# A two-layer attention block and feed-forward: new orders for the first and last periods, feed-forward weights loaded elsewhere in the period, output weight rows in 12 transfers

## The reference

```
h1 = layernorm(x);  x = attention(h1, h1)      @ o1 + o1_b + x     # "own" attention, keys 100
h2 = layernorm(x);  x = attention(h2, context) @ o2 + o2_b + x     # "cross" attention, keys 361
h3 = layernorm(x);  a, g = split(h3 @ ff_w1 + ff_b1)               # 320 -> 2 x 1280
out = (a * gelu(g)) @ ff_w2 + ff_b2 + x                            # 1280 -> 320
```

## Time and profile before

| | |
|---|---|
| median of 3 runs | 1327.53 us (1322.02 to 1328.48) |
| the profiled execution, its own time | 1335.46 us |
| its span, first to last instruction | 1333.7 us |
| TensorE busy (matmul) | 1248.4 us, 94% of the span |
| VectorE, ScalarE, GpSimd busy | 62%, 50%, 45% |
| mean granted TensorE clock | 0.971 |
| stages (from the trace) | first stage to 150.1, lead-in to 199.0, 29 periods to 891, run-out to 973.4, feed-forward to 1333.7 us |

### The profile page before, as it was taken

The page is one execution under the profiler, slowest core; times in us unless marked ns, Lnnn a source line. Parts: engine busy times, 40 slices in busy tenths (PEclk is TensorE's granted clock), DMA queues, the critical chain, the costliest instruction groups (busy, mean ns, idle before and its releaser), DMA issues. The chain is left out here.

```text
span 1333.7 us, 34303 instructions
## 1 busy us (share of the span) xinstructions
PE 1248.4 (94%) x12788; PEld 1168.4 (88%) x12788; DVE 826.6 (62%) x1606; ACT 672.8 (50%) x1622; POOL 602.7 (45%) x792
## 2 busy tenths in 40 slices
PE   6999679999999999999999999998689999999999
PEld 4899578899988898888889999987589999999999
DVE  5645458888787787777787888875445333242521
ACT  5655236666665666656666666664343232313131
POOL 5521225555555554544655555541366342333331
PEclk9999789999999999999999999998689999999999
DMA  4576644545545555445454554533011101010000
GB/s 125 192 250 231 184 144 124 157 135 149 162 129 161 162 150 181 145 140 179 135 155 142 146 164 128 171 100 87 13 55 41 45 1 50 0 49 0 25 1 25
DMA packets 105865, 154.49 MB, mean 116 GB/s; under 512 B 21500, under 2 KB 87284, under 8 KB 105716
## 3 DMA queue, kind: packets, MB, share of 16 engines
q1 hardware_dynamic: 105716, 152.49, 37.4%
HBM read 62.98 MB, written 28.93 MB: 69 GB/s over the span
## 5 line engine op out<-in xcount | busy, mean ns | idle before, releaser
L1419 ACT ACTIVATE probs<-expin 120x400 f32<-120x400 f32 (+2 forms) x635 | 297.4, 506 | 133.1 <-PE expin L812 130.2
L1096 DVE TENSOR_REDUCE neg_max<-score 100x2 f32<-100x722 f32 x320 | 287.7, 899 | 105.9 <-PE score L786 104.7
L812 PE MATMUL expin<-qs,ks 128*120 128x200 f32 (+2 forms) x1270 | 201.4, 273 | 1.2 <-ACT probs L1419 0.9
L786 PE MATMUL score<-ks,qs 128*100 128x362 f32 x640 | 170.3, 348 | 29.4 <-DMA qs<-q_parts 13.8
L812 PEld LDWEIGHTS expin<-qs,ks 128*120 128x120 f32 (+2 forms) x1270 | 180.4, 183 | 11.3 <-ACT probs L1419 7.8
L2654 DVE SCALAR_TENSOR_TENSOR hidden<-ps_a,b_cols,gelu 128x320 f32<-128x320 f32 x100 | 55.0, 550 | 174.2 <-PE ps_a L2578 174.1
L1610 POOL MEMSET qs<- 128x2400 f32 (+1 forms) x58 | 112.6, 1942 | 94.9 <-PE expin L812 94.9
L2816 POOL TENSOR_TENSOR hid_lo<-hidden,hid_hi 128x320 fp32r<-128x320 f32 x100 | 88.2, 882 | 121.8 <-ACT hid_hi L2724 121.6
L190 POOL TENSOR_TENSOR scaled_heads<-turned_heads,rden 128x320 f32<-128x320 f32 x63 | 48.0, 762 | 190.2 <-DVE rden L195 190.2
L786 PEld LDWEIGHTS score<-ks,qs 128*100 128x100 f32 x640 | 87.4, 168 | 50.0 <-issue 40.2
L2736 ACT ACTIVATE gelu<-ps_g,b_cols 128x320 f32<-128x320 f32 x100 | 52.8, 528 | 137.6 <-PE ps_g L2578 137.6
(11 more groups left out here) (222 smaller groups left out, 2971.0 us busy)
## 6 DMA issues: line engine op xcount, KB each, us to landing
ks<-kc_parts SPq DMA_DIRECT2D x96, 362.0 KB, 3.7
qk_dram<-qk_parts SPq DMA_DIRECT2D x32, 500.0 KB, 5.3
qs<-q_parts SPq DMA_DIRECT2D x192, 75.0 KB
ks<-qk_dram SPq DMA_DIRECT2D x96, 125.0 KB
ctx_raw<-in_ctxT SPq DMA_DIRECT2D x64, 180.5 KB
ks<-kc_parts SPq DMA_DIRECT2D x96, 90.5 KB, 2.7
qs<-qk_dram SPq DMA_DIRECT2D x64, 125.0 KB
v_dram<-v_rows SPq DMA_DIRECT2D x32, 132.8 KB
```

The costliest lines, as they stand in the source:

```text
L786: mm = pe.matmul(score[0:N, a, 0:JP], qs[2][u][:, a, q_slot(c), :], ks[2][u][:, k_slot(c), :], start=True, stop=True)
L812: mm = pe.matmul(dst, ks[a][u][:, k_slot(c) if a == 2 else c, j0:j0 + n], qs[a][u][:, :, q_slot(c) if a == 2 else c, :], start=True, stop= ...
L1096: ins = nc.vector.tensor_reduce(dst, src, AX_X, ALU.max, negate=True)
L1419: nc.scalar.activation(probs[e % NPT][0:n, :], expin[e % 2][0:n, 0:HG * N], ACT.Exp, scale=SCALE)\
```

## The change

Nothing that is computed changes. Four things are done:

1. `rows_of_heads`: the rows of o1 and o2 go to the same places in 12 transfers of 32 partitions (40 KB), not 24 of 16 (20 KB).
2. `lead_in` has another order on all five engines, and `FILL_WORK` with it.
3. `load_w1` is issued inside the period, behind `place_max(2, x)`, not at its end. The rest of the period is as before.
4. `run_out` has another order on all five engines, and `DRAIN_WORK` with it.

```diff
 def rows_of_heads(w):
     pieces = []
-    for k, f0, step in ((0, 0, 4 * DH), (2, P, 4 * DH), (1, 2 * P, 0)):
-        for i in range(HG):
-            for half in range(2):
-                f = f0 + half * step + DH * i
-                pieces.append((BLK * i + DH * half, k, w[f:f + DH]))
+    for i in range(HG):
+        r = slice(DH * i, DH * (i + 1))
+        pieces += [(BLK * i, k, w[f:f + P].rearrange("(h r) m -> h r m", h=2)[:, r]) for k, f in ((0, 0), (2, P))]
+        pieces.append((BLK * i, 1, w[2 * P:D][r].unsqueeze(0).broadcast_to([2, DH, D])))
     return pieces
...
                 place_q2(s)
                 place_max(2, x)
+                if x is not None and 8 <= x < 8 + FF // P:
+                    load_w1(x - 8)
                 load_context(f)
...
             for p in PERIODS:
                 period(*roles(p), p + 4 if p + 4 < B else None)
-                if 8 <= p < 8 + FF // P:
-                    load_w1(p - 8)
```

SyncE's lists:

```diff
             def lead_in():
+                load_qkv1(2)
                 set_key_rows()
-                load_x(1)
+                place_max(1, 1)
                 load_context(1)
-                load_x(2)
-                place_max(1, 1)
-                load_qkv1(2)
                 place_kc(0, 0)
                 place_q2(0)
+                load_x(1)
+                load_qkv1(3)
+                place_max(1, 2)
+                load_x(2)
+                place_kc(0, 2)
                 load_context(2)
-                place_kc(0, 2)
+                place_kc(1, 0)
                 load_x(3)
-                place_max(1, 2)
-                load_qkv1(3)
-                place_kc(1, 0)
             def run_out():
                 place_q2(30)
                 place_max(2, 29)
                 place_kc(30, 2)
-                store_x2(27)
                 place_kc(31, 0)
                 place_q2(31)
                 place_max(2, 30)
+                load_tiles()
                 place_kc(31, 2)
-                load_tiles()
+                store_x2(27)
```

GpSimd's `run_out`:

```diff
-                second_residual(31)
                 clear_cross(31)
                 scale_products(2, 29)
                 heads_low(2, 29)
+                second_residual(31)
+                pool.wait_ge(max_made, SCORE_AT[2, B - 1, HP - 1] + 1)
+                tile_deviation(0)
+                split_piece(0)
+                tile_deviation(1)
+                split_piece(1)
                 scale_products(2, 30)
+                tile_deviation(2)
+                split_piece(2)
                 heads_low(2, 30)
-                pool.wait_ge(max_made, SCORE_AT[2, B - 1, HP - 1] + 1)
-                for i in range(3):
-                    tile_deviation(i)
                 scale_products(2, 31)
                 heads_low(2, 31)
-                for i in range(EARLY):
-                    split_piece(i)
```

More of the change, by code:

```diff
@@ L857, in lead_in @@
                 self_scores(1, 0)
+                project_out(1, 0)
+                project_vc(0, 0)
                 self_scores(1, 1)
+                project_vc(0, 1)
                 turn_max(1, 1)
+                turn_normalised(0)
                 project_kc(0, 0)
                 project_kc(0, 1)
-                project_out(1, 0)
-                turn_normalised(0)
-                project_kc(0, 2)
-                project_q2(0)
-                turn_q2(0)
-                scores_for_exp(1, 1, 0, 0)
-                project_vc(0, 0)
-                project_vc(0, 1)
-                self_scores(2, 0)
-                scores_for_exp(1, 1, 1, 0)
+                project_q2(0)
+                self_scores(2, 0)
+                turn_q2(0)
+                project_vc(0, 2)
+                scores_for_exp(1, 1, 0, 0)
+                scores_for_exp(1, 1, 1, 0)
+                project_kc(0, 2)
                 scores_for_exp(1, 1, 2, 0)
-                project_vc(0, 2)
                 scores_for_exp(1, 1, 3, 0)
+                self_scores(2, 1)
                 scores_for_exp(1, 1, 4, 0)
-                self_scores(2, 1)
                 times_v(1, 1, 0)
@@ L881, in lead_in @@
                 times_v(1, 1, 4)
+                project_kc(1, 0)
+                turn_max(1, 2)
                 cross_scores(0, 0)
-                turn_max(1, 2)
                 cross_scores(0, 1)
-                project_kc(1, 0)
                 cross_scores(0, 2)
+                project_out(1, 1)
+                cross_scores(0, 3)
                 project_kc(1, 1)
-                cross_scores(0, 3)
-                project_out(1, 1)
                 cross_scores(0, 4)
@@ L915, in run_out @@
                 times_v(1, 31, 4)
+                project_out(2, 28)
                 cross_scores(30, 0)
-                project_out(2, 28)
                 scores_for_exp(2, 29, 0, 0)
-                cross_scores(30, 1)
                 scores_for_exp(2, 29, 0, 1)
@@ L1007, in run_out @@
                 scores_for_exp(2, 31, 4, 2)
[L1008 removed]
                 times_v(2, 31, 3)
[L1010 to L1011 removed]
                 times_v(2, 31, 4)
                 turn_tile(2)
+                project_out(2, 30)
                 project_out(2, 31)
@@ L1222, in lead_in @@
                 maximum(1, 1, 0)
+                second_input(0)
+                statistics(0)
                 maximum(1, 1, 1)
+                normalise(0)
                 max_low(1, 1)
+                features_low("T2", 0)
                 kc_low(0, 0)
                 kc_low(0, 1)
-                second_input(0)
-                statistics(0)
-                normalise(0)
-                features_low("T2", 0)
-                kc_low(0, 2)
                 q2_low(0)
@@ L1250, in lead_in @@
                 maximum(2, 0, 6)
+                kc_low(1, 1)
+                maximum(2, 0, 7)
+                q2_low(1)
+                maximum(2, 0, 8)
+                maximum(2, 0, 9)
                 kc_low(1, 2)
-                maximum(2, 0, 7)
-                maximum(2, 0, 8)
-                q2_low(1)
-                maximum(2, 0, 9)
             def run_out():
@@ L1309, in run_out @@
                 tile_low(2)
+                result(29)
+                result(30)
                 result(31)
@@ L1840, in head_rows @@
                 for p0, k, src in rows_of_heads(w):
-                    sp.dma_start(dst[p0:p0 + DH, k, :], src).then_inc(done, 16)
+                    sp.dma_start(dst[p0:p0 + 2 * DH, k, :], src).then_inc(done, 16)
             def all_rows(dst, v, done):
```

200 lines of the change are left out of this document (100 added, 100 removed).

## The result

The changed kernel takes 1304.82 us (median of 4 runs, 1303.07 to 1306.6), the kernel before 1328.01 in the same session (4 runs, 1322.02 to 1328.72). The ratio is 0.9835, interval 0.9804 to 0.9867: 23 us or 1.7% faster. The forecast was 1287, with a range up to 1303.

The account below looks back on a forecast made before the run. TensorE was taken as busy nearly throughout, with idle time at the ends and behind ff_w1 loads. Terms 3.7 + 9.3 + 12.0 + 19.4 = 44.4 us off 1335.46 gave 1291.1; median forecast 1287, range 1275 to 1303.

Parts of the forecast that it names:

- Output weight rows: First stage: fewer issues let the value store start earlier and TensorE's 2.03 us wait go; 3.7 us, bounds 0 and 4.
- wide transfers: Rival, first stage: the 40 KB transfers are slow, so the first term falls from 3.7 to 0: 1291 us; chance 0.07.
- Lead-in: Lead-in: new order hides the chain of the normalised rows and brings `place_q2` earlier; 9.3 us, bounds 5 and 12.
- The second half: Lead-in from first cross score to first period: 18.3 us instead of 21.1, a gain of 2.8.
- ff_w1 loads: Periods: loads issued in a queue gap no longer delay the query stack; gain 12.0 us, bounds 8 and 12.
- Run-out: End of the stage: new order on all engines brings feed-forward earlier; gain 19.4 us, 12.4 at half clock, bounds 10 and 21.
- (b): Run-out: GpSimd clears the stack of 31 about 2.5 us earlier; its first score starts about 914.3, not 916.41.
- (c): Run-out: ten scores of 31 alternate with maxima at 1.57 us a score; the maximum is there at about 930.6.
- (d): Run-out: the maximum's transfer is covered by exponents and a projection; exponents of 31 start at 934.6, not 940.71.
- e to g: Run-out: exponents, covered weight pieces, then last projection and heads; feed-forward starts at 954 at full clock, 961 at half.
- the rival of half rate: Rival, run-out tail: TensorE stays at half clock in the last exponents, 7 us less gain: 1294 us; chance 0.25.
- From the profile to the median: Whole kernel: median before is 7.9 us below the profiled execution; unknown whether that goes or stays, so 4.0 taken off.

Follow-up runs that it names:

- x rows first: Changed kernel with the context 1 load first in SyncE's lead-in, plus x rows of tiles 16 to 19 issued ahead of the twelve output weight transfers: 1303.1 us.
- half the transfers: Changed kernel with the context 1 load first in SyncE's lead-in, and half of the first twelve output weight transfers moved to group 3: 1297.9 and 1300.2 us.
- the single experiment: Kernel before with only the output weight rows in 12 transfers: 1327.3 us, ratio 0.9974.
- the early context: Changed kernel with the load of context 1 ahead of everything in SyncE's lead-in: 1301.5 and 1303.2 us, ratios to before 0.9736 and 0.9727.
- two experiments that agree: Kernel before with only the ff_w1 loads moved: 1322.3 us; changed kernel with the loads at their old place: 1316.7 us, 8.7 slower than changed.
- single parts of session 2: Kernel before with one part each: loads moved 0.9924, 12 transfers 0.9974, new lead-in 1.0003, new run-out 0.9870, as ratios to before.

## Why the prediction was wrong

The sign, the periods and the mechanism of the run-out were right. The gain was forecast at 40.4 us and is 23.2. The sum of the terms, 44.4, measured 32.4 between the two profiled executions (12.0 less: 3.1 in the output weight rows, 6.6 in the lead-in, 0.4 in the loads, 2.5 in the run-out, and feed-forward 0.6 the other way); of these, 9.2 do not appear in the medians, where I had taken off 4.0. 12.0 + 9.2 - 4.0 is the miss of 17.2. The range had a slip of its own: 49 off 1335.46, and then the whole 7.9, is 1278.5, so its lower end of 1275 does not come out of its sum. At the upper end of 1303 no case had the lead-in fall below its bound of 5.

- **Output weight rows, 3.7 forecast.** In the traces 0.6. The store "then starts up to 6.3 earlier, its data being long made" failed twice: the issue of a wide transfer takes 0.8, not 0.52 to 0.65, and ahead of the store stand the x rows, which I had not followed. ("First stage: one wait" was short of one too: TensorE also waits 1.35 us before values at 125.22, and no part of the change touches that.) The rival "wide transfers" looked at the transfers alone ("8.3 for twelve, 2 behind the issues; the term would then stay whole"), and not at who is queued behind them. Shown by three places of the same transfers: x rows first moves the wait to the values, half the transfers removes it. That it is the two DMA engines which hold up what follows is argued. The median of the single experiment is 3.7 all the same, which is luck as far as the forecast's working goes; in the changed kernel the 24 are no slower. What gives the 3.7 alone is not settled; its trace points to the clock in the lead-in.
- **Lead-in, 9.3 forecast, 2.7 in the two traces, 1.5 as a mean of profiles, 1.1 and 1.6 alone in the medians of two sessions, neither clear of none.** This is the step that failed most: "`load_qkv1(2)` now opens the queue: six microseconds of issues, done by 158, hidden by the same chain". I counted its issues and not its wait for the stored values, so it begins at 154.34 and is done at 159.8; behind it the maximum and then the context are late, the context takes 8 us to be there (163.25 to 171.32), and its key projection stands ahead of the first cross score on TensorE. The chain on TensorE that I had followed was right to 0.4 us, up to the query transpose; SyncE's arrival at `place_q2` was not (166.47 for 164.0). With the load of the context ahead of that wait, lead-in and load give 10.4 us by the medians, the forecast's size, but 5.5 as a mean of profiles: in the profile with the early context SyncE still reaches `place_q2` at 165.62, 16.7 us into the lead-in where the forecast had 13.9, because `load_qkv1(2)` waits as before. So of the miss of 6.6 the late context is the larger part (4.0), and the 2.8 by which SyncE is still late fit the rest. The second half measured 18.85 for 18.3.
- **ff_w1 loads, 12.0 forecast.** 11.6 in the two traces (675.1 us before and 663.5 after, from the lead-in's end to the last mark), 10.2 as a mean of profiles, 8.7 to 10 in the medians of two experiments that agree. The working was right; the loss in the profiled execution was larger than in most.
- **Run-out, 19.4 forecast, 16.9 in the traces, 15.6 to 17.3 alone.** Against the forecast's own times, from the last mark: the first score of 31 comes 0.65 us earlier, not 2.1 (b); from it to the maximum 17.1, not 16.3 (c); from there to the exponents 3.8 for 4.0 (d); from these to feed-forward 19.9 for 19.4 (e to g). The steps add up to the 2.5 that lack. The step that failed is (b) with (c), the time of the last maximum. Against the profile of before it came 3.4 earlier and not 5.65; and in that profile it stood later than in any other with the old order (62.2 us behind the last mark, 59.4 to 61.1 in five). Over all profiles it is 60.4 before and 59.8 after, so this step is worth 0.6, and the 13.2 of the mean come from the tail (4.6 from the maximum to the last product) and the pieces (7.9 from there to feed-forward). That the clock stays up in the tail was right in all twelve profiles with a new run-out (0.90 to 1.00), and the rival of half rate wrong. The pieces are covered, as forecast; alone they are worth 3.5 in the medians and 6.1 in the profile.
- **From the profile to the median, 4.0 forecast, 9.2 measured.** I said that no row tells whether the 7.9 us lie in what goes or in what stays. They lay largely in what goes: in the profiled execution of before the run-out is 2.5 above the mean of six profiles and the loss by the loads 1.6 above the mean of seven. These are 4.1 of 7.5; that of after was 1.75 below its own median. By the table of means the four terms are 25.8, 6 less than between the two profiled executions; the other 3 of the 9.2 are open, and so is why the kernel before differs by 11 us over five sessions and the changed kernel by 4 over three.

The single parts of session 2 multiply to 0.977. The changed kernel had 0.9835, 0.9788 and 0.9833. If the wide transfers are worth nothing within it, that accounts for 0.0026, where the difference is 0.0016 to 0.0063; by the intervals of the parts the product is uncertain by some 0.005 (my estimate), so whether the parts act on each other is not told.

## What to carry to other kernels

When an instruction list is reordered, walk the queue's list as carefully as the engine's: for each entry its own wait, then the landing of everything behind it, and ask of a transfer with few DMA engines who is next in the queue and not how long it takes itself. When a stall is taken out of a list, the next one is often in a different queue; here the move of one load was worth 7 to 9 us in the medians (4 in the profiles), and the whole new order of the lead-in without it nothing that the medians show. And take the size of a stall from several executions where it can be had: a term read from one profile, in stretches where the clock or transfers vary, is a sample.

## What the runs showed of the hardware

- Twelve transfers of 32 partitions and 40 KB kept a share of 0.13 of the 16 DMA engines busy at 47 GB/s and took 0.8 us each to issue (24 of 20 KB 0.52). VectorE got the rows issued behind them 7.8 us after their issue, behind the 24 after 2.3.
- A wait for stored values to land in DRAM ended 5.3 us after the last of the stores was issued (149.0 to 154.34).
- The same instructions at the end of the old run-out ran at a granted clock of 0.50 to 0.89 in six executions; the stretch from the last mark to feed-forward took 92.9 to 99.4 us.
- The time of an identical kernel differed by up to 11 us between sessions, 0.8%, while the changed one differed by 4 in three of them.
